# A batched residual product in split fp32: batches 2 to 6 laid out in contiguous quadrants, T of a batch in four transfers, and another order of the first unit

## The reference

```python
def reference(x, itok_B_1_98, L0_cond_T):      # x: 8 x 512 x 512, T: 100 x 512 x 512, fp32
    def _L0_cond_ref(x, fwd_steps, T):
        Tb = T[fwd_steps - 1]
        return jnp.einsum('bij,bjk->bik', Tb, x)
    x = x + _L0_cond_ref(x, itok_B_1_98, L0_cond_T)
    return x
```

## Time and profile before

| | |
|---|---|
| median of 3 runs (lowest, highest) | 103.46 us (102.8, 105.82) |
| the profiled execution: time, span | 102.88 us, 101.1 us |
| busy: PE, DVE, ACT, POOL | 95.7, 87.0, 65.4, 73.1 us |
| granted TensorE clock, mean | 0.997 |
| moved by DMA | 25.30 MB, mean 250 GB/s |

### The profile page before, as it was taken

One profiled execution on the slowest core, in us unless ns is written; L12 is line 12 of the kernel. 1 busy time (PEld: TensorE's weight loads), 2 busy tenths in 40 slices (PEclk: granted clock), 3 DMA queues, 4 the chain that ended last, 5 costly groups with the idle time before them and its releaser, 6 DMA issues.

```text
span 101.1 us, 1833 instructions
## 1 busy us (share of the span) xinstructions
PE 95.7 (95%) x440; PEld 79.2 (78%) x440; DVE 87.0 (86%) x101; ACT 65.4 (65%) x87; POOL 73.1 (72%) x38
## 2 busy tenths in 40 slices
PE   3999999999999999999999999999999999999950
PEld 3996888888888888887887888888888888888840
DVE  0168889999999999989999999999999999993250
ACT  0957598858585969677676767696867768462100
POOL 2004199999979797978989898989797989908100
PEclk9999999999999999999999999999999999999998
DMA  2899798889999879999999999999999782505074
GB/s 58 288 309 389 191 276 221 257 237 333 302 305 282 264 173 341 252 274 325 246 348 285 319 221 351 217 313 288 284 321 283 250 302 67 211 0 207 6 286 129
DMA packets 22125, 25.30 MB, mean 250 GB/s; under 512 B 2402, under 2 KB 16994, under 8 KB 22114
## 3 DMA queue, kind: packets, MB, share of 16 engines
q10 hardware_dynamic: 4850, 15.34, 47.6%
q1 hardware_dynamic: 17264, 9.84, 36.6%
HBM read 16.78 MB, written 8.39 MB: 249 GB/s over the span
## 4 chain that ended last, share of the span: by engine, by line
PE 87%; DMA 5%; SPq 3%; issue 0%; DVE 0%
PE same L470 29%; PE same L459 28%; PE diff L481 28%; DMA T_sb<-T 5%; SPq L170 2%; PE turned L444 2%; SPq L155 1%; PE diff L491 1%; PE same L491 0%; DVE out_sb L415 0%
## 5 line engine op out<-in xcount | busy, mean ns | idle before, releaser
L302 POOL TENSOR_TENSOR xL<-x_sb,xH 128x1024 fp32r<-128x1024 f32 x14 | 33.8, 2416 | 6.2 <-ACT xH L211 6.1
L318 POOL TENSOR_TENSOR TD_r<-TH_r,TL 128x1024 fp32r<-128x1024 f32 x14 | 33.9, 2420 | 4.1 <-issue 3.7
L470 PE MATMUL same<-xL,TL 128*128 128x512 f32 x128 | 34.6, 392 | 0.0
L459 PE MATMUL same<-xH,TH_r 128*128 128x512 f32 x128 | 34.4, 391 | 0.0
L481 PE MATMUL diff<-xD,TD_r 128*128 128x512 f32 x124 | 33.2, 390 | 0.0
L247 ACT ACTIVATE diff<-same 128x512 f32<-128x512 f32 x31 | 18.1, 583 | 22.4 <-PE same L470 15.8
L358 DVE STREAM_TRANSPOSE turned<-T_sb 128x512 f32<-128x512 f32 x28 | 29.7, 1110 | 0.6 <-DMA T_sb<-T 0.4
L459 PEld LDWEIGHTS same<-xH,TH_r 128*128 128x128 f32 x128 | 23.9, 188 | 5.4 <-ACT TH_r L225 0.3
L470 PEld LDWEIGHTS same<-xL,TL 128*128 128x128 f32 x128 | 23.7, 188 | 5.2 <-DVE TL L380 0.3
L481 PEld LDWEIGHTS diff<-xD,TD_r 128*128 128x128 f32 x124 | 23.3, 188 | 4.9
L388 DVE TENSOR_TENSOR out_sb<-x_sb,diff 128x512 f32<-128x512 f32 x31 | 21.5, 693 | 3.9 <-PE diff L481 3.9
(11 more groups left out here) (29 smaller groups left out, 21.0 us busy)
## 6 DMA issues: line engine op xcount, KB each, us to landing
out<-out_sb ACTq DMA_DIRECT2D x15, 512.0 KB, 6.3
T_sb<-T SPq DMA_DIRECT2D x112, 64.0 KB, 4.9
x_sb<-x ACTq DMA_DIRECT2D x13, 512.0 KB, 5.9
x_sb<-x SPq DMA_DIRECT2D x2, 512.0 KB, 6.0
x_sb<-x ACTq DMA_DIRECT2D x2, 256.0 KB, 2.8
T_sb<-T SPq DMA_DIRECT2D x2, 256.0 KB, 4.7
T_sb<-T SPq DMA_DIRECT2D x1, 512.0 KB, 6.3
out<-out_sb SPq DMA_DIRECT2D x1, 256.0 KB, 2.6
```

Source lines behind the costliest of these rows:

```text
L302: nc.gpsimd.tensor_tensor(half(xL, h), x_sb[b % X_SLOTS][:, i:i + 2], half(xH, h).bitcast(fp32), ALU.subtract).then_inc(xL_ready, 2)
L318: nc.gpsimd.tensor_tensor(TD_r[s][:], TH_r[s][:].bitcast(fp32), TL[s][:].bitcast(fp32), ALU.subtract).then_inc(TD_ready, 2)
L459: nc.tensor.matmul(same[U % 2][:], TH_r[p][:, i, j], xH[s][:, j], start=(j == 0), stop=False)
L470: done = nc.tensor.matmul(same[U % 2][:], TL[p][:, i, j], xL[s][:, j], start=False, stop=(j == N - 1))
```

## The change

The start: ACT loads only x's tiles 0 and 1 and the indices; SP loads T's first block, then x's tiles 2 and 3 in a transfer each, then the rest of T. `WARM` falls from 10 to 2. xD of the first half is made from xH directly, ahead of the first TL; the copy through PSUM is made for the second half. T's third and fourth block of unit 0 are turned into `xH_copy`, so unit 1's turn needs no wait for TL. TensorE multiplies unit 0 by tiles: high and low with tiles 0 and 1, with 2, then turns unit 1, then high and low with tile 3.

Batches 2 to 6 (`QUADS`): partition 32g + c holds rows 128g + 32u + c, so that a quadrant of 32 partitions is one contiguous 256 KB of HBM, moved in rows of 2 KB. x comes in four transfers from SP, one semaphore for all; out goes in four from ACT once the whole batch is summed, two in each of two pairs. T's rows are taken in the same order, which makes VectorE's turn read neighbouring elements. For batches 3 to 6 (`WHOLE`) T comes in four transfers of 256 KB, one semaphore for all four blocks. Batch 7 keeps the layout of before, with x in one transfer.

```diff
-    FIRST_X = [(0, 1), (1, 2), (2, 4)]
-    WARM = 10
+    QUADS = range(2, B - 1)
+    WHOLE = range(3, B - 1)
+    WARM = 2
...
+    x_quad = x.rearrange("b (g u c) k -> b g c u k", u=N, c=Q)
+    out_quad = out.rearrange("b (g u c) k -> b g c u k", u=N, c=Q)
...
+    T_quad = T.rearrange("t (m n q) (g c) -> t n g q m c", n=N, q=Q, g=G)
+    T_whole = T.rearrange("t (s q) (g c) -> t g q s c", q=Q, g=G)
...
-                        (turned[:, 1, 2:4], slice(2, 4))]
+                        (xH_copy[:, 0, 2 * P:4 * P].rearrange("p (j i) -> p j i", j=2), slice(2, 4))]
...
+            if b in WHOLE:
+                return {0: (N, G)}
...
+        def load_first_x(eng, u):
+            eng.dma_start(x_sb[0][:, u], first_x_part[:, u]).then_inc(first_x_loaded[u], 16)
...
+        def load_x(eng, b):
+            if b not in QUADS:
+                eng.dma_start(x_sb[b % X_SLOTS][:], x_part[b]).then_inc(x_loaded[b % X_SLOTS], 16)
+                return
+            for g in [0, 2, 1, 3]:
+                eng.dma_start(x_sb[b % X_SLOTS][g * Q:(g + 1) * Q], x_quad[b, g]).then_inc(x_loaded[b % X_SLOTS], 16)
...
+        def T_view(s):
+            return T_sb[s][:].rearrange("p a d -> p (a d)").rearrange("p (m n d) -> p n m d", m=G, n=N)
...
+                if b in WHOLE:
+                    for g in [0, 2, 1, 3]:
+                        eng.dma_start(T_sb[s][g * Q:(g + 1) * Q].rearrange("q a d -> q (a d)").rearrange("q (s c) -> q s c", c=P),
+                                      T_whole[bass.ds(t, 1), g].rearrange("a q s c -> (a q) s c")).then_inc(T_loaded[s][n], 16)
+                    continue
...
+        def store_quad(eng, b, g):
+            eng.dma_start(out_quad[b, g], out_sb[b % OUT_SLOTS][g * Q:(g + 1) * Q]).then_inc(stored[b % OUT_SLOTS], 16)
...
             t = matrix(itok_row[0:1, 0:1])
-            load_T(sp, t, 0)
-            load_x_half(sp, 2)
+            load_T(sp, t, 0, range(1))
+            load_first_x(sp, 2)
+            load_first_x(sp, 3)
+            load_T(sp, t, 0, range(1, N))
+            load_second_x(sp, 0)
             sp.wait_ge(itok_loaded, 16)
             t = matrix(itok_sb[0:1, 1:2])
             load_T(sp, t, 1, range(2))
-            load_x_half(sp, 3)
+            load_second_x(sp, 1)
             load_T(sp, t, 1, range(2, N))
-            load_T(sp, matrix(itok_sb[0:1, 2:3]), 2)
-            for b in range(T_SLOTS, B):
+            for b in range(2, B):
+                if b >= X_SLOTS:
+                    sp.wait_ge(sum_ready, (b - X_SLOTS + 1) * N)
+                load_x(sp, b)
                 t = matrix(itok_sb[0:1, b:b + 1])
-                wait_turned(sp, (b - T_SLOTS + 1) * N)
+                if b >= T_SLOTS:
+                    wait_turned(sp, (b - T_SLOTS + 1) * N)
                 load_T(sp, t, b)
...
-                act.wait_ge(half_x_loaded[b % X_SLOTS][h % 2], 16 * (b // X_SLOTS + (1 if b % X_SLOTS else 0)))
+                if b == 1:
+                    act.wait_ge(half_x_loaded[h % 2], 16)
+                else:
+                    act.wait_ge(x_loaded[b % X_SLOTS], 16 * sum(x_transfers(c) for c in range(2, b + 1) if c % X_SLOTS == b % X_SLOTS))
...
-                if h:
-                    act.wait_ge(xD_ready, 2 * h)
+                act.wait_ge(xD_ready, 2 * h)
+                if h == 1:
+                    act.wait_ge(TL_ready, 1)
...
-            for done, (u, end) in zip(first_x_loaded, FIRST_X):
-                act.dma_start(x_sb[0][:, u:end], first_x_part[:, u:end]).then_inc(done, 16)
+            load_first_x(act, 0)
+            load_first_x(act, 1)
             act.dma_start(itok_sb[:], itok_row).then_inc(itok_loaded, 16)
-            for u in range(N):
-                cut_first_x(u)
+            cut_first_x(0)
+            cut_first_x(1)
             cut_first_T()
-            copy_xH_half(0)
+            cut_first_x(2)
+            cut_first_x(3)
             cut_T(1)
+            copy_xH_half(1)
             seed(0)
             cut_T(2)
+            cut_T(3)
             cut_x_half(2)
-            cut_T(3)
             seed(1)
             copy_xH_half(2)
             cut_x_half(3)
...
-            load_x_half(act, 4)
             for k in range(1, PAIRS):
-                b = k // 2
                 seed(2 * k)
                 for h in x_halves(k):
                     cut_x_half(h)
                 for p in T_pairs(k):
                     cut_T_pair(p)
-                if k + 4 < 2 * B:
-                    if b >= 2:
-                        act.wait_ge(sum_ready, (b - 1) * N)
-                    load_x_half(act, k + 4)
                 seed(2 * k + 1)
                 for h in copied_halves(k):
                     copy_xH_half(h)
-                if k < PAIRS - 1:
+                b = (k - 1) // 2
+                if b not in QUADS and b < B - 1:
                     act.wait_ge(sum_ready, 2 * k)
-                    store(act, (k - 1) // 2, slice(2, N) if k % 2 == 0 else slice(0, 2), stored[(k - 1) // 2 % OUT_SLOTS])
+                    store(act, b, slice(2, N) if k % 2 == 0 else slice(0, 2), stored[b % OUT_SLOTS])
+                b = (k - 2) // 2
+                if b in QUADS and (k % 2 == 0 or b < B - 2):
+                    act.wait_ge(sum_ready, (b + 1) * N)
+                    for g in [0, 2, 1, 3] if b == B - 2 else [0, 2] if k % 2 == 0 else [1, 3]:
+                        store_quad(act, b, g)
...
-                if U == 1:
-                    pool.wait_ge(xD_ready, N)
+                if U == 0:
+                    pool.wait_ge(first_xL_ready, N)
...
-                if h != 1:
-                    dve.wait_ge(xH_copied, max(h, 1))
+                if h:
+                    dve.wait_ge(xH_copied, h)
                 if h // 2 >= X_SETS:
                     dve.wait_ge(diff_ready, (h // 2 - X_SETS + 1) * N)
-                high = half(xH, h).bitcast(fp32) if h == 1 else xH_copy[:]
+                high = xH_copy[:] if h else half(xH, h).bitcast(fp32)
...
+                if b in QUADS:
+                    blocks = T_view(b % T_SLOTS)[:, n].rearrange("p m (u c) -> p m u c", c=Q)
+                else:
+                    blocks = T_sb[b % T_SLOTS][:, n].rearrange("p (m c u) -> p m u c", c=Q, u=N)
+                nc.vector.transpose(turned[:, U % 2].rearrange("p u (m q) -> p m u q", q=Q), blocks).then_inc(turned_by_dve, 1)
...
-            for u in range(N):
-                first_xL(u)
+            first_xL(0)
+            first_xL(1)
+            cut_x_half(0)
             cut_first_T()
-            cut_x_half(0)
+            first_xL(2)
+            first_xL(3)
             cut_T(1)
             cut_x_half(1)
             cut_T(2)
+            cut_T(3)
             turn(4)
-            cut_T(3)
             turn(5)
             sum_up(0)
...
+                if N - 1 in tiles:
+                    done.then_inc(same_ready, 1)
...
-            multiply_high(0)
+            multiply_high(0, [0, 1])
+            multiply_low(0, [0, 1])
+            multiply_high(0, [2])
+            multiply_low(0, [2])
             turn(1)
-            multiply_low(0)
+            multiply_high(0, [3])
+            multiply_low(0, [3])
             multiply_high(1)
             turn(2)
```

More of the change, by code:

```diff
@@ L130, in T_transfers, with x_transfers, stores @@
                 return {0: (1, 1), 1: (2, 1), 2: (N, 1)}
+            if b in WHOLE:
+                return {0: (N, G)}
             return {n: (n + 1, G) for n in range(N)}
+        def x_transfers(b):
+            return G if b in QUADS else 1
+        def stores(b):
+            return G if b in QUADS else 2
         def wait_T_loaded(eng, U):
@@ L194, in _ @@
             for s in range(OUT_SLOTS):
-                sp.wait_ge(stored[s], 32 * ((B - 2 - s) // OUT_SLOTS + 1))
+                sp.wait_ge(stored[s], 16 * sum(stores(c) for c in range(s, B - 1, OUT_SLOTS)))
         @block.scalar
@@ L445, in turn, with multiply_high @@
                 done.then_inc(turned_by_pe, 1)
-            def multiply_high(U):
+            def multiply_high(U, tiles=range(N)):
                 b, n = U // N, U % N
@@ L451, in multiply_high @@
                     pe.wait_ge(seeded, U - 1)
-                for j in range(N):
+                for j in tiles:
                     if U == 0 and j < 2:
@@ L459, in multiply_high, with multiply_low @@
                     nc.tensor.matmul(same[U % 2][:], TH_r[p][:, i, j], xH[s][:, j], start=(j == 0), stop=False)
-            def multiply_low(U):
+            def multiply_low(U, tiles=range(N)):
                 b, n = U // N, U % N
```

29 lines of the change are left out of this document (15 added, 14 removed).

## The result

The changed kernel takes 108.0 us (median of 6 runs, 106.3 to 110.1) beside 103.5 for the kernel before on the same chip: a ratio of 1.031 with a 95% interval of 1.024 to 1.037. All ratios here compare only executions within 1.5% of the fastest of their kernel, so this one rests on 106.3 and 106.7; by the medians of all six it is 1.044. It is slower; 102.6 with a range to 104.4 was forecast. The profiled execution took 107.95 us, with a span of 106.2 (101.1 before). All six executions had a mean granted clock of 0.992 or more, so the clock has no part in this result, nor in the spread of nearly 4 us between them; in some of the experiments it has a part.

What follows compares the result with a forecast made beforehand. TensorE was taken to bound the loop, with VectorE, SyncE and DMA close behind. From the profiled 102.88 us, head -0.2 and loop waits -0.35 gave 102.3; the median likewise 102.9; forecast between, 102.6 us, range 101.3 to 104.4.

Steps and rivals of the forecast that it cites:

- The head: Start, before the loop: unit 1's low product starts near 12.2 us instead of 12.38, -0.2 us, bounds +0.1 and -0.5.
- The turn: VectorE's transpose of T, batches 2 to 6: 0.6 us instead of 0.99 with neighbouring reads; no difference in the sum.
- idle 0.7 us a pair: Loop, expected sign: VectorE, with shorter turns, stands idle 0.7 us per pair of units, waiting for TensorE.
- T in four transfers: Loop, batches 3 to 6: fewer SyncE issues remove the loop's waits, -0.35 us, bounds 0 and -0.36.
- others come: Loop: the reason given for the bound 0 on T's step, that other waits replace those removed.
- Quadrant stores and x loads: Loop: the new form moves the DMA from just enough to enough; no gain on the path, since nothing there waits.
- the other three: Loop: VectorE, SyncE's issues and the DMA engines, nearly as slow as TensorE; freeing them returns at most 0.35 us.
- x of batch 2 comes late: Rival, early loop: x follows batch 1's T on SyncE; a 1 us miss gives 103.3 to 104.4; chance 0.13.
- Quadrants are slower: Rival, loop: quadrant transfers reach half the ports; at 265 GB/s, below the 290 needed, +3, near 106; chance 0.10.
- 259 GB/s at 15 to 16 us: Evidence against slow quadrants: before's rate with supposedly only T's quadrant pieces in flight, over half of any full rate seen.

Runs made afterwards that it cites:

- b_head: The kernel before with the edits of the head alone, the loop as before: 103.6 us, ratio 0.999.
- d_T16: The kernel before with the head's edits and the contiguous row order, T of batches 3 to 6 still in 16 transfers: 103.3 us, ratio 0.993.
- d_wide: The kernel before with the head's edits, contiguous row order and T of batches 3 to 6 in four transfers; x and stores as before: 107.9 us, ratio 1.021.
- d_outquad: d_wide with stores of batches 2 to 6 in quadrants, two after a batch's last sum and two a pair later: 107.8 us, ratio 1.039.
- a_x3: The changed kernel with batch 3's four x loads issued by ACT at pair 2, about 7 us earlier, instead of SyncE: 107.7 us, ratio 1.031.
- a_wide: The changed kernel with x of batches 2 to 6 in transfers of the same size, each over all 128 partitions instead of 32: 107.4 us.
- d_xquad: d_wide with x of batches 2 to 6 in quadrants, all four issued by ACT where the first half was: 106.0 us, ratio 1.025.
- e_mended: The changed kernel with T in 16 transfers, x quadrants issued by ACT, and all four stores of a batch together after its last sum: 106.6 us.
- b_T4: The kernel before with the head's edits and T of batches 3 to 6 in four transfers, row order as before: 108.5 us, ratio 1.029.

## Why the prediction was wrong

**The head, right.** "-0.2 us" came as -0.13 to low(1), all its marks within 0.1 but the first piece of TL (6.73, forecast 7.2); the same head in b_head's profile gave -0.5, the forecast's lower bound, and lost it again; b_head measured 0.999.

**The turn, right.** Two turns in d_T16 take 1.22 us, 0.61 each (forecast 0.6; rows in the last section), worth little on the path, as the sum had it: d_T16's ratio is 0.993 and b_head's 0.999. VectorE's idle 0.7 us a pair came too (d_T16: 6.6 us in ten waits for TH).

**"T in four transfers: -0.35 us, bounds 0 and -0.36".** This is the step that failed. I costed the operation by what it spares SyncE, and never asked what the first consumer now waits for. In its place stand +2.4 us at full clock (d_wide against d_T16), and more where TensorE falls to half clock after the stall. The sign was to be had from before's trace: SyncE's 16 issues of a batch take 11.0 us, as the prediction says, so a whole T is there long after its first block. The 0.4 us of the earlier trace rows, which I counted as a gain, are the turn of the fourth block at 43.95 and mark when the whole of T was there; the batch's first turn ran 6.9 us before. The bound "0" had no more behind it than the words "others come".

**"Quadrant stores and x loads: no gain on the path", and so a cost of nothing.** The second failed step: the stores' place was moved by a pair, and what waits for them (VectorE's first sum two batches later) isn't in the text. The changed kernel's trace has 1.6 us at that place, d_outquad's 0.4, and its time 1.3 beyond d_wide's. x's move belongs to the same step: ACT's cut does wait for x, and the changed kernel's trace has 3.5 us behind that wait.

These prices can't be summed to 108.0. T in four costs 2.4 us where nothing else is late, yet its wait in the changed kernel's trace is 0.5 us, since x's stall ahead of it gave T the time to land. What is shown is that T in four alone brings most of the loss, and that neither removing x's stall, nor the stores', nor T in four from the changed kernel brings the time back. How the loss divides among them there stays open.

**"TensorE is the bound, and freeing the other three can return 0.35 us, no more."** True for gains, and I used it as if it held for losses. TensorE has no slack to repay a gap, whatever resource caused it; and a transfer can be late for its first consumer while its queue is no busier than before.

**Rival "x of batch 2 comes late" (0.13, up to 1 us).** Its mechanism appeared, a batch later and larger: ACT waited 3.7 us for batch 3's x, where 16 transfers of T stood ahead in the queue; I had worked through the first batch in the new order and not the second. It carries 3.5 us in the profiled execution, but it is not the only way to lose them: a_x3 takes it away and VectorE waits for T instead.

**Rival "Quadrants are slower" (0.10, near 106).** It named the time, and its rate is there (226 to 248 GB/s). The Trainium skill, "SBUF — State Buffer", section "Door 1: The DMA port swizzle", gives partitions 0 to 31 half of the ports. The rows don't settle whether that is at work: with T and x in quadrants the engines are fully busy at 226 to 248 GB/s, but before, with x at full width, shows 234 in the earlier trace rows too. My evidence against it, 259 GB/s at 15 to 16 us, was such a rate and not a refutation; nor were only quadrants in flight then, since the full-width half of batch 1's x, issued at 11.46, landed 4.2 us later. Its sum had a slip as well: at 272 GB/s a batch takes 11.6 us, and by the rival's own working that is +1.5 us, not 2%, which it passes near 269. a_wide moved the time by nothing measurable, and d_T16, whose T is in quadrants of 64 KB, has no loss. d_xquad isn't such evidence, since its own stall took the place of T's. For the changed kernel the form is not shown to be a cause; e_mended, 3.3 us slow with T by units, leaves it open.

## What to carry to other kernels

When transfers are merged, write down for each what its first consumer needed before and needs now, and compare the moment when the whole of it lands with the moment of the first use; here the saved issues were the smaller half of the account. When several resources are within a few per cent of the bound, the wait that a trace shows is only the latest of several late arrivals: removing it proves nothing until the time moves. Here one-part tests from the side of the kernel before found a cause that repairs of the changed one had not. Even then, an early stall lends time to every later transfer, so parts that are each harmful alone can look free together.

## What the hardware showed that was unexpected

A full-width transfer whose memory view has 4 as its outermost dimension ran at 100 GB/s with a DMA share of 0.2; batch 0's stores, a view of 128 x 2 x 512, ran while 343 GB/s moved in all. How a transfer is dealt out was not tried further.

VectorE's transpose of 512 fp32 takes 0.61 us reading neighbours and 0.99 reading every fourth; d_T16's timeline:

```profile
64.68 1.31 DVE L411 STREAM_TRANSPOSE turned<-T_sb 128x512 f32<-128x512 f32 x2
65.90 1.20 DVE L400 SCALAR_TENSOR_TENSOR xD<-xL,xH_copy 128x1024 fp32r<-128x1024 f32 x1
```

After stalls of about 2 to 5 us TensorE sometimes came back at half clock. In b_T4, after a gap of 2.4 us beyond the usual distance (last three numbers PEclk, DMA share, GB/s):

```profile
44.00:45.00 1.00, 1.00 (x3) 0.81 (x4) 1.00 (x2) 0.66 (x2) 0.00 (x0) 0.50 1.21 234
45.00:46.00 1.00, 1.00 (x4) 0.72 (x3) 1.00 (x3) 0.86 (x1) 0.48 (x1) 0.50 1.21 227
```

0.50 is the level of 1.2 GHz; seven matmuls there stand 0.43 us apart, not 0.23: 1.4 us. The three groups of four from 43.83 to 48.20 take 4.4 us where 2.7 is usual: 1.6 in all. In d_wide the four executions with a mean clock of 0.976 to 0.984 took 107.8 to 108.5 us and the two at full clock 105.3 and 106.0; that is 2.5 us, so those four may have had longer stalls too; they have no trace. In the profiled execution of the changed kernel a gap of 3.2 us had no such tail (PEclk 1.00 in its rows above). So a stall can cost more than half as much again, or not; what decides it wasn't found.
